# Router logits of a cross-attention and mixture-of-experts kernel from split parts, in another buffer and another order

## The reference

```
q = layernorm(x) @ W_q;  k = ctx @ W_k;  v = ctx @ W_v          8 heads of 64
x = x + softmax(where(mask, q k^T / 8, -max)) v @ W_o + b_o
xf = layernorm(x)
probs = softmax(xf @ Wr)                                        Wr is 512 x 8
top 2 of 8 experts per token; per expert the 1120 best tokens:
y[idx] += gate * (relu(xf[idx] @ W1[e]) @ W2[e])
x = x + y
```

## Time and profile before

| | |
|---|---|
| runs | 2064.83 us median of 3 (2063.95 to 2065.74) |
| profiled execution | 2064.88 us, of which the span of instructions 2063.1 us |
| busy, share of the span | TensorE 95%, VectorE 49%, ScalarE 35%, GpSimd 23% |
| chain that ended last | TensorE 69%, nearly all in the experts |
| L775, products of lg0 | 64 records for 32 products, 576 ns mean |
| L677, copy of a tt | 32, 617 ns mean |
| L829, turns of lt0 | 32 records for 32 transposes, 198 ns mean |

### The profile page before, as it was taken

One profiled execution on the slowest core, in us unless ns is written; L12 is line 12 of the kernel. 1 busy time (PEld: TensorE's weight loads), 2 busy tenths in 40 slices (PEclk: granted clock), 3 DMA queues, 4 the chain that ended last, 5 costly groups with the idle time before them and its releaser, 6 DMA issues.

```text
span 2063.1 us, 30182 instructions
## 1 busy us (share of the span) xinstructions
PE 1951.8 (95%) x11419; PEld 1730.5 (84%) x11419; DVE 1005.7 (49%) x2471; ACT 718.4 (35%) x1928; POOL 477.1 (23%) x560
## 2 busy tenths in 40 slices
PE   4799999999849999999999999999999999999997
PEld 3688888888638888998888888888998988889996
DVE  5678888887676353334133413442343353236221
ACT  3556776666414133123112311331132132115111
POOL 2445565455510021011001100111101011112101
PEclk9899999999959999999999999999999999999999
DMA  6112332221144144124112421341143144115102
GB/s 183 33 53 64 87 87 64 69 55 42 54 137 148 16 117 124 15 51 143 48 15 51 142 48 16 92 133 31 25 132 84 16 109 115 31 21 162 32 6 27
DMA packets 96316, 148.40 MB, mean 72 GB/s; under 512 B 8608, under 2 KB 50096, under 8 KB 96160
## 3 DMA queue, kind: packets, MB, share of 16 engines
q1 hardware_dynamic: 80288, 109.41, 16.9%
q0 software_dynamic: 15872, 36.71, 10.0%
HBM read 110.70 MB, written 35.39 MB: 71 GB/s over the span
## 4 chain that ended last, share of the span: by engine, by line
PE 69%; DVE 1%; issue 1%; POOL 0%; POOLq 0%; ACT 0%; DVEq 0%
PE psH L1713 33%; PE psY L1713 31%; PE psY L1752 2%; PE psX L1727 1%; PE psI L1775 1%; DVE w_lo L1128 0%; PE psI L1765 0%; POOL out_dram L1497 0%; POOLq L1409 0%; DVE hT_lo L1687 0%; PE psI L1781 0%; DVE moves L1563 0%; DVE onehot L1571 0%; DVE slot_tile L1648 0%; DVE ys L1646 0%
## 5 line engine op out<-in xcount | busy, mean ns | idle before, releaser
L1687 DVE SCALAR_TENSOR_TENSOR hT_lo<-psH,hT_hi 128x384 fp32r<-128x384 f32 (+1 forms) x384 | 209.7, 546 | 868.1 <-ACT hT_hi L1527 529.0
L1527 ACT ACTIVATE hT_hi<-psH 128x384 fp32r<-128x384 f32 (+1 forms) x384 | 185.2, 482 | 1064.0 <-PE psH L1713 1064.0
L1713 PE MATMUL psH<-xgT_hi,w_hi 128*128 128x256 f32 (+3 forms) x1536 | 477.4, 311 | 10.7 <-issue 9.9
L1713 PE MATMUL psH<-xgT_hi,w_lo 128*128 128x256 f32 (+3 forms) x1536 | 476.4, 310 | 2.2 <-issue 2.2
L1713 PE MATMUL psH<-xgT_lo,w_hi 128*128 128x256 f32 (+3 forms) x1536 | 475.0, 309 | 1.7 <-issue 1.7
L1713 PE MATMUL psY<-w_hi,hT_hi 128*128 128x512 f32 (+1 forms) x921 | 371.7, 404 | 0.0
L1713 PE MATMUL psY<-w_lo,hT_hi 128*128 128x512 f32 (+1 forms) x921 | 362.7, 394 | 1.2 <-issue 1.2
L1713 PE MATMUL psY<-w_hi,hT_lo 128*128 128x512 f32 (+1 forms) x921 | 362.2, 393 | 0.0
L1713 PEld LDWEIGHTS psH<-xgT_hi,w_hi 128*128 128x128 f32 x1536 | 291.1, 190 | 37.4 <-issue 20.5
L1713 PEld LDWEIGHTS psH<-xgT_lo,w_hi 128*128 128x128 f32 x1536 | 291.4, 190 | 14.7
L1713 PEld LDWEIGHTS psH<-xgT_hi,w_lo 128*128 128x128 f32 x1536 | 291.1, 189 | 4.3 <-issue 4.3
(11 more groups left out here) (227 smaller groups left out, 2867.4 us busy)
## 6 DMA issues: line engine op xcount, KB each, us to landing
stage<-in_L_ffn_W_dram SPq DMA_DIRECT2D x128, 512.0 KB, 4.6
x_sb<-in_x_dram SPq DMA_DIRECT2D x8, 896.0 KB, 5.7
x_res<-in_x_dram SPq DMA_DIRECT2D x8, 896.0 KB, 5.5
out_dram<-x_res SPq DMA_DIRECT2D x8, 896.0 KB, 4.8
xn_rows<-xn SPq DMA_DIRECT2D x8, 896.0 KB, 4.8
c_sb<-in_ctx_dram SPq DMA_DIRECT2D x8, 384.0 KB, 6.1
c_sb<-in_ctx_dram SPq DMA_DIRECT2D x32, 96.0 KB, 5.6
out_dram<-zrow SPq DMA_DIRECT2D x9, 256.0 KB, 4.1
```

The lines of the kernel that those rows point to most:

```text
L1527: h = nc.scalar.activation(hT[0][:, f % 2, 0:m], psH[f % 2][:, 0:m], ACT.Relu)
L1687: h = nc.vector.scalar_tensor_tensor(out=hT[1][:, f % 2, 0:m], in0=psH[f % 2][:, 0:m], scalar=0.0, in1=f32(hT[0][:, f % 2, 0:m]), op0=ALU. ...
L1713: mm = nc.tensor.matmul(out, stationary(a, c), moving(b, c), start=first and c == chunks[0] and j == 0, stop=last and c == chunks[-1] and ...
```

## The change

Ahead of the loop ScalarE and VectorE split `Wr` into high and low parts, side by side as 16 columns (`wr_parts`). tt0 to tt3 are split like fx, high part by ScalarE and low part by VectorE, and go into `xT`, the buffer of the first normalisation's transposes. lg0 becomes eight float32r products of 448 columns that yield 16 rows, 8 for each part of `Wr`. lt0 turns them with `add_parts` (two identity matrices of 8, one above the other) in place of the identity, which adds the two groups of rows. As `xT` is read by q3 of the pair and written by fx0 of the next, the steps tt0 to tt3 now stand behind q3, and fx0 to fx3 behind lg0. `x2T` is left to the loading of weights.

```diff
@@ -178,24 +178,24 @@
 PE_STEPS = order("""
-    t-3 q1 s0 k1 o-4 t-2 o-3 s1 s2 t-1 v0 s3 q2 o-2 o-1 t0 wo0 wo1 s4 v1 wo2 t1 v2 o0 v3 s5 o1 tt0 t2 t3
-    s6 s7 tt1 wo3 o2 t4 k2 o3 q3 t5 s8 k3 o4 t6 s9 s10 fc0 o5 tt2 t7 s11 tt3 fx0 o6 fx1 t8
-    s12 lg0 o7 fx2 t9 lt0 s13 o8 fc1 t10 fc2 o9 t11 s14 fx3 s15 k0 q0 o10 o11 t12
+    t-3 q1 s0 k1 o-4 t-2 o-3 s1 s2 t-1 v0 s3 q2 o-2 o-1 t0 wo0 wo1 s4 v1 wo2 t1 v2 o0 v3 s5 o1 t2 t3
+    s6 s7 wo3 o2 t4 k2 o3 q3 t5 s8 tt0 k3 o4 tt1 t6 s9 s10 fc0 o5 tt2 t7 s11 tt3 o6 t8 lg0
+    s12 fx0 o7 t9 lt0 fx1 s13 fx2 o8 fc1 t10 fc2 o9 t11 s14 fx3 s15 k0 q0 o10 o11 t12
 """)
 ACT_STEPS = order("""
     o-4 t-3 q1 k1 t-2 o-3 s0 v0 t-1 o-2 q2 o-1 s1 t0 s2 v1 s3 o0 v2 t1 v3 o1 t2 s4 s5 t3 s6 o2 t4 k2 o3
-    s7 q3 t5 k3 s8 o4 fc0 t6 o5 t7 s9 fx0 fx1 t8 s10 s11 fx2 t9 o6 s12 fc1 fc2 o7 t10 t11 fx3 o8 o9
+    s7 q3 t5 tt0 k3 s8 o4 tt1 t6 fc0 o5 tt2 t7 s9 tt3 t8 s10 s11 fx0 t9 o6 fx1 s12 fx2 fc1 fc2 o7 t10 t11 fx3 o8 o9
     s13 k0 o10 s14 q0 o11 t12 s15
 """)
 DVE_STEPS = order("""
     s0 t-3 o-4 q1 s1 k1 t-2 fs0 fs1 t-1 o-3 v0 o-2 fs2 fs3 q2 o-1 s2 wo0 fa0 wo1 t0 s3 o0 v1
-    s4 wo2 fp0 ap0 ap1 t1 v2 s5 v3 tt0 ap2 o1 t2 fp1 tt1 o2 fp2 s6 t3 wo3 t4 s7 k2 fp3 o3
-    s8 ap3 o4 q3 t5 k3 s9 fc0 tt2 t6 tt3 s10 fx0 s11 t7 s12 fx1 o5 o6 lg0 t8 lt0 fx2 t9
-    s13 fc1 fc2 t10 o7 fx3 s14 o8 s15 t11 o9 k0 mb0 o10 q0 t12 o11
+    s4 wo2 fp0 ap0 ap1 t1 v2 s5 v3 ap2 o1 t2 fp1 o2 fp2 s6 t3 wo3 t4 s7 k2 fp3 o3
+    s8 ap3 o4 q3 t5 tt0 k3 s9 tt1 t6 fc0 s10 tt2 s11 t7 tt3 s12 o5 o6 lg0 t8 lt0 fx0 fx1 t9
+    s13 fx2 fc1 fc2 t10 o7 fx3 s14 o8 s15 t11 o9 k0 mb0 o10 q0 t12 o11
 """)
@@ -221,12 +221,12 @@
-ACT_END = order("t-3 o-4 t-2 o-3 t-1 o-2 o-1")
+ACT_END = order("t-3 o-4 t-2 o-3 t-1 o-2 o-1 tt0 tt1 tt2 tt3")
-SPLIT = ("fx", "fc", "v", "q", "k")
+SPLIT = ("fx", "fc", "v", "q", "k", "tt")
@@ -312,7 +313,7 @@
-        lgT = sb("lgT", [E, TP * R])
+        lgT, wr_parts, add_parts = sb("lgT", [2 * E, TP * R]), sb("wr_parts", [128, DCH, 2, E], F32R), sb("add_parts", [2 * E, E])
@@ -501,6 +507,9 @@
+                elif kind == "tt":
+                    nc.scalar.activation(xT[0][:, :, i * R:(i + 1) * R], src[:, 0:DCH * R].rearrange("p (c r) -> p c r", c=DCH),
+                                         ACT.Copy).then_inc(proj_hi, 1)
@@ -557,6 +566,8 @@
             iteration(0, False, True)
+            act.wait_ge(T["b_in"], 32)
+            nc.scalar.activation(wr_parts[:, :, 0, :], T["wr"][:], ACT.Copy).then_inc(wr_hi, 1)
             with act.Fori(1, NPAIR - 1) as p:
@@ -569,6 +580,9 @@
+                elif kind == "tt":
+                    a, h, o = (src[:, 0:DCH * R].rearrange("p (c r) -> p c r", c=DCH), xT[0][:, :, i * R:(i + 1) * R],
+                               xT[1][:, :, i * R:(i + 1) * R])
@@ -671,14 +685,10 @@
-                    elif kind == "tt":
-                        dve.wait_ge(proj_mm, ring(p, prev, nxt, "tt", i) + 1)
-                        src = bank(p, prev, nxt, "tt", i)[:, 0:DCH * R].rearrange("p (c r) -> p c r", c=DCH)
-                        nc.vector.tensor_copy(x2T[:, :, i * R:(i + 1) * R], src).then_inc(proj_done, 1)
...
-                        nc.vector.tensor_copy(lgT[:], src[0:E, 0:TP * R]).then_inc(lg_copied, 1)
+                        nc.vector.tensor_copy(lgT[:], src[0:2 * E, 0:TP * R]).then_inc(lg_copied, 1)
@@ -704,6 +714,9 @@
             iteration(0, False, True)
+            dve.wait_ge(wr_hi, 1)
+            nc.vector.tensor_tensor(wr_parts[:, :, 1, :], T["wr"][:], f32(wr_parts[:, :, 0, :]), ALU.subtract).then_inc(wr_done, 1)
+            nc.vector.tensor_tensor(add_parts[:], T["ident"][0:2 * E, 0:E], T["ident"][0:2 * E, E:2 * E], ALU.add).then_inc(add_done, 1)
@@ -772,7 +785,9 @@
                     pe.wait_ge(proj_done, ring(p, prev, nxt, "tt", TP - 1) + 1)
                     for c in range(DCH):
-                        mm = nc.tensor.matmul(out[0:E, 0:TP * R], T["wr"][:, c, :], x2T[:, c, :], start=c == 0, stop=c == DCH - 1)
+                        for k in range(2):
+                            mm = nc.tensor.matmul(out[0:2 * E, 0:TP * R], wr_parts[:, c].rearrange("p k e -> p (k e)"), xT[k][:, c, :],
+                                                  start=c == 0 and k == 0, stop=c == DCH - 1 and k == 1, skip_group_check=True)
@@ -826,7 +841,8 @@
-                            mm = nc.tensor.transpose(out[0:R, TP * R + t * E:TP * R + (t + 1) * E], lgT[:, t * R:(t + 1) * R], ident[0:E, 0:E])
+                            mm = nc.tensor.matmul(out[0:R, TP * R + t * E:TP * R + (t + 1) * E], lgT[:, t * R:(t + 1) * R], add_parts[:],
+                                                  start=True, stop=True, skip_group_check=True)
@@ -834,7 +850,8 @@
             iteration(0, False, True)
-            pe.wait_ge(T["b_in"], 32)
+            pe.wait_ge(wr_done, 1)
+            pe.wait_ge(add_done, 1)
             with pe.Fori(1, NPAIR - 1) as p:
```

More of the change, by code:

```diff
@@ L268 @@
 HITER = sum(k in SPLIT for k, _ in ring_order(True, True))
+HFIRST = sum(k in SPLIT for k, _ in ring_order(False, True))
 assert (NPRO + NFIRST) == NITER and NITER % 2 == 0
@@ L331, in attention_short @@
         passed = sem("passed")
+        wr_hi, wr_done, add_done = sem("wr_hi"), sem("wr_done"), sem("add_done")
         w_in, w_hi, w_lo = [sem(f"w_in{i}") for i in range(NS)], sem("w_hi_done"), sem("w_lo_done")
@@ L355, in hi_count @@
                 return PRO_ORDER.index((kind, i)) + 1
-            return [x for x in ring_order(prev, nxt) if x[0] in SPLIT].index((kind, i)) + 1 + NPRO + HITER * p
+            at = [x for x in ring_order(prev, nxt) if x[0] in SPLIT].index((kind, i)) + 1 + NPRO
+            if not prev:
+                return at
+            last = len([x for x in OF_NEXT if x[0] in SPLIT]) if isinstance(p, int) and p == NPAIR else 0
+            return at + HFIRST - HITER - last + HITER * p
         def v_half(src, h):
```

## The result

The changed kernel took 2106.64 us (median of 4 runs, 2105.38 to 2107.11) beside 2065.28 us for the kernel before on the same chip (4 runs, 2063.95 to 2068.91): a ratio of 1.0202, interval 1.0187 to 1.0217. Forecast were 2108 us and slower. The profiled execution took 2107.11 us with a span of 2105.1, 42.0 more than before.

| stretch | before, us | after, us | difference | predicted |
|---|---|---|---|---|
| start to the end of pair 0's products | 107.10 | 107.47 | +0.4 | 0 |
| from there to s0 of pair 1 | 5.40 | 10.58 | +5.2 | +3.5 to +4 |
| s0 to the first logits | 52.66 | 54.73 | +2.1 | |
| five periods of the loop | 314.81 | 344.29 | +29.5 | |
| the last pair | 61.70 | 69.04 | +7.3 | |

A forecast was written before the change was run, and what follows sets the result against it. TensorE's written order plus its waits was taken as the bound. Six pairs at +5.0, last pair +2, entry +4, tail -1.0 made +35; with the clock's +8.5, 43.5 over 2064.88 us: forecast 2108, range 2076 to 2124.

The forecast's parts named there:

- What bounds: Attention loop: a pair takes TensorE's written order plus its waits, 62.94 us with TensorE busy 61.84.
- The products: TensorE, each pair: lg0 falls from 3.11 to 1.65 us, lt0 rises from 0.31 to 0.6; net gain 1.2.
- The stalls: TensorE, each pair: k3 2.65, fc0 0.85, lg0 1.6, lt0 with fx1, fc1, fc2 1.7; sum 6.8 us.
- The entry: After pair 0, once: TensorE waits for Wr's split ahead of the loop, +4 us with the clock.
- The last pair: Last pair, without fc and fx: only k3 and lg0 stall, estimated +2 us.
- The tail: Tail: lg0 gains 2.0 us, less 0.7 for ScalarE's hop and 0.3 for lt0; -1.0 us.
- The clock: Five of seven k3 stalls are followed by 3.41 us at half clock, 1.7 lost each: +8.5 us.
- Rival 3: TensorE's clock holds, as the stalls stay short enough: 2100 us; chance 0.15.
- Rival 1: Loop: only k3's wait lasts, later releases being early: 2073 us, with the clock 2082; chance 0.16.
- rival 2: The clock stays low for longer, 6.83 us as in the tail: 2124 us; chance 0.13.
- rival 4: Faster: q3's release is early enough, so the 1.2 us of products per pair come through: 2055 us; chance 0.05.
- rival 5: Even: products gain nothing, or stalls are half as long and the clock holds: 2061 to 2069 us; chance 0.03.

The follow-up runs named there:

- e1: The changed kernel's order of steps alone, with the old copies, fp32 products, turn and buffers of the kernel before; 2111.51 us, ratio 1.0234.
- e2: The changed kernel's new arithmetic in two buffers of its own, with TensorE's old order of steps; 2063.95 us, ratio 1.0008.
- e5: The changed kernel with k3 again ahead of tt0 and the steps behind it spread out, same buffers; 2103.52 us, ratio 1.0192.
- e6: e2 with the wait ahead of the loop moved to lg0 and o6, s12, o7 spread behind tt3; 2057.62 us, ratio 0.9966.
- e4: The changed kernel with 17 unused products behind each tt0 but the last pair's, filling k3's wait; 2098.36 us, ratio 1.0175.
- e3: The changed kernel with TensorE's wait for the parts of Wr moved from ahead of the loop to lg0; 2103.48 us, ratio 1.0191.

## Why the prediction was right, step by step

- **What bounds.** Right: a pair takes TensorE's written order and its waits. e1 puts the loss on the order, and e2 takes it away with the order. Only "busy TensorE near 61" did not come: 61.9 in e5 at full clock.
- **The products.** lg0 1.65, as forecast. lt0 0.85 from start to start in the last pair (0.88 in e6) where 0.6 was put, so the gain is 0.9 a pair, by e1 and e4 too, not 1.2.
- **The stalls.** k3 2.41 for 2.65, fc0 0.75 for 0.85, lg0 1.33 for 1.6; lt0, fx1, fc1 and fc2 together (1.4 + 1.7 + 3.8) / 4 = 1.7 in e4, as put, though by luck in its parts: lt0 0.35 for 0.1, fc1 and fc2 0.95 for 1.15. Sum 6.2 for 6.8. As a whole the order costs 6.05 a pair (e1 at full clock, 69.01 against 62.96) where 6.8 - 0.5 = 6.3 were put. Less gain and smaller stalls nearly cancel: 5.13 a pair at full clock for 5.0.
- **The entry.** t-3 started at 113.80 (113.1 put), and from it to s0 passed 4.25 us where 3.0 were put, at half clock from 109.90 to 116.73; so s0 was 5.2 us late, not 3.5. e3 shows 3.7 of it left at the first logits (4 put).
- **The last pair.** Mis-sized: of its +7.3, 1.4 are stalls of fx1, fc1 and fc2 behind the lt0 before it, which stood in the sixth 5.0, and two falls at 0.64 make 1.3; 4.6 are left against the +2. k3's 2.41 and lg0's 1.85 (1.6 put), less 0.9 for the products, are 3.4 of them. No wait of tt2 was to be saved there, so by the prediction's own terms, 2.65 + 1.6 - 1.2, the +2 was too small. I did not split the rest.
- **The tail.** lg0's records span 3.15 us where they had 5.28, but its wait is 1.39 for 0.81, and lt0, behind the same wait of 0.8, takes 1.6 at half clock. From lt0's start to the copy of the logits it is 1.67 us, before 0.40: +1.3 where 0.3 was put, so the tail gains 0.4 and not 1.0.

```profile
617.61 0.53 PE L789 MATMUL psJ<-xT_hi,wr_parts 128*16 128x448 f32 x1 [1.39 <-DVE xT_lo L603]
...
621.55 1.63 PE L844 MATMUL psJ<-add_parts,lgT 16*112 16x8 f32 x8 [0.80 <-DVE lgT L691]
```

- **The clock.** Five of seven stops of k3 were followed by 3.41 us at half clock, as put. The price was not 1.7 but 0.64 on average, and four more falls came behind shorter stops: nine at 0.64 make 5.8 for 8.5, two errors against each other. That it was just five is luck: the prediction had only three stops of before to go by, and e1, with the same stops of 2.41 us, stayed at 1.00 through the two pairs shown. Rival 3, that the clock holds, is out for this kernel. e5, with no stop over 1.71 in its loop, ran at 1.00 from its second pair on, and e4's four periods at 1.00 are how that rival would have gone, 0.77 us a pair shorter. The Trainium skill (TensorE: Matmul & The Clock Gate, section "Why this matters for your kernels") warns, in that section, only of gaps longer than any in the loop; the falls after 2.41 and 1.85 us, and after the short stops of lt0 and fx1, don't agree with it. The stop of 6.05 us at the entry is of the length it warns of, and the 6.83 us at half clock there do agree.
- **Rival 1**, that only k3's wait lasts, failed on the waits of lg0, fx1 and fc; **rival 2** on the length of the falls (3.41 us each in the loop); **rival 4** on the split of q3, which ended at 227.42, 3.7 us after t5 had begun (1.2 were needed); **rival 5** on lg0's 1.65 and the 6.2 us of stalls.
- **The sum.** That 2108 was met to 1.4 us is in part luck: the clock's 2.7 us less and 2.0 less in the experts, which the forecast had at nothing, stand against 2.6 more in the last pair and 0.6 more in the tail.

## What to carry to other kernels

An operand put into a buffer that another step still reads is an order, not only a saving of memory: count how many steps it forces behind that last read, and follow each through the ring and through the lists of the engines that split it, since moving one of them can only move the wait (e5, 68.2 us for e4's 68.1, part of it by the lists of ScalarE and VectorE). Products saved on the busiest engine were worth nothing here while the engines that feed them had more to do (e2, e6). A stop's second price, the lower clock, was smaller than its length says where the next waits took it up (0.64 for 1.7 us).

## What the runs showed that was not expected

A stationary of 16 columns takes the same time as one of 128: eight products in 1.65 us, 0.206 each, and q3's 0.207. Four fp32 products of 8 columns leave eight records and hold TensorE 0.85 to 0.88 us, 0.1 a record; lg0's eight old records, with 56 times the columns, took 3.11 us, 0.39 each. A fall of the clock to half for 3.41 us cost 0.64 on average, not 1.7, and three came when the last stops had been 0.35 and 0.43 us and a longer one lay 6 to 7 us back. And the experts' stage, whose code is the same, differs by up to 10.5 us between these profiles, which alone decides between e6 and the kernel before.
